# The node sum of a graph's values: seven adds on GpSimd and one product instead of eight, in the next feed-forward

## The chip, the cores and the metric

One NeuronCore of a Trainium2 chip runs the whole program. The metric is device time of one execution in microseconds (us); the median of three runs is taken. The engines are TensorE (PE; its weight loads are PEld), VectorE (DVE), ScalarE (ACT), GpSimd (POOL) and SyncE (SP), which issues the DMAs.

## What is computed

Eight graphs of 1024 nodes with 256 features go through a three-layer graph transformer (L0), and then through one graph-attention layer (L1). Cut to what matters here:

```python
h = relu(layernorm(x))
x = x + L0(h, adj)                 # 3 layers: masked attention, layernorm, feed-forward, layernorm
h = relu(layernorm(x))
# L1:
Wh = h @ W
e = leaky_relu((Wh @ a1)[:, :, None] + (Wh @ a2)[:, None, :])
e = where(adj == 0, -1e9, e)
h_prime = softmax(e, axis=2) @ Wh
x = x + elu(h_prime)
```

In L1 a node may have no edge at all. All its scores are then equal, and its row of the softmax is a plain mean over the 1024 nodes. The kernel needs for this the sum of `Wh` over all nodes of a graph, a row of 256 numbers that stands in every partition: the node sum. It is added where a node has no edge.

## The kernel before, in words

The nodes of a graph lie in 8 tiles of 128 partitions. The work is 32 steps, one layer of one graph each, in the order of the table `ORDER`: steps of L0 are feed-forward steps (`ffn_step`), steps of L1 are `gat_step`. Each engine has its own program, which walks through the steps in the same order; inside a step the order is written out by hand by tables (`prep_tables`) and conditions on `t` (the tile, 0 to 7) and `n` (the feed-forward iteration, 0 to 15). The engines wait for one another through semaphores. No scheduler moves anything.

A feed-forward step has two parts. In the first, for `t` in 0 to 7, TensorE makes `aggregate` (8 products of f32, 128x257, each recorded in two halves, so x16 in the trace) into the banks `OB`, and VectorE makes `residual1` (L1105, L1109) and the LN1 statistics. GpSimd turns statistics into factors (`ln_rstd`, L621 to L629), ScalarE normalises (L822), and after tiles 3, 5 and 7 TensorE transposes pairs of tiles (L1636). In the second, for `n` in 0 to 15, TensorE makes `hidden` (6 products, up-projection, two iterations ahead) and `second` (12 products, down-projection into `OB`), ScalarE the GELU (L853) and its upper half (L858), and the lower half is made by VectorE for even `n` (L1242) and by GpSimd for odd `n` (L657). At the end VectorE adds the residual (`residual2`, L1122) from `OB`, which frees the banks for the first `aggregate` of the next step, makes the LN2 statistics (L1095, L1098), and splits the columns of scores (L1168 to L1174). GpSimd makes the LN2 factors and `affine` (a multiply L644 and an add L646 per tile, 128x256 f32); those of tiles 4 to 7, `tail`, stand at the start of its next step.

In the shadow of a step other work is done: scores of the next step (`unit` on TensorE, 4 products with `nms`; `score` on VectorE, L1228; exponentials on ScalarE, L864), masks, row maxima (L1204), and the preparation of a graph for L1 (`GAT_AT`: the step in which it is prepared). For graph 0 that is step 5, for graphs 1 to 5 steps 8, 12, 16, 20 and 24, for graph 6 step 28, for graph 7 the `gat_step` 29. `gat_product` makes `Wh`, `gat_values` writes it to `xx` (signal `wv_done`), `scores` on VectorE (L1146 and L1151) reduce it with `a1` and `a2`: two inputs in SBUF, 128x256, one instruction each.

The node sum of a graph is `gat_colsum` on TensorE: eight products of a matrix of ones with the eight tiles of `xx`, f32, summed in the bank `TP`. It stands at `n == 14`, ahead of `second(k, 14)`. `gat_sum` on VectorE (L1284) copies it into `csum`, after the LN2 statistics at the end of the step. It is read by `elu_a` (L1299) in the `gat_step` of that graph, at step 6 for graph 0 and one to five steps after the preparation for the others.

Of the kernel before, what the change touches and what calls it, by code (L numbers as in the profile page):

```python
# [37 lines left out]
BATCH, N, D = 8, 1024, 256  # L38
LAYERS, FF = 3, 1024
NT = N // P  # L40
# [46 lines left out]
GAT_FFN_LATE = {5}  # L87

# [102 lines left out]
def build(nc, x, adj, attn_w, attn_b, W1, b1, W2, b2, g1, beta1, g2, beta2, gatW, gata, out):  # L191
# [10 lines left out]
    with ctx:  # L202
# [143 lines left out]
        cs_done = sem("cs_done")  # L346
        wct_done = sem("wct_done")
# [243 lines left out]
        def _(pool):  # L591
# [89 lines left out]
            def ffn_step(k):  # L681
# [29 lines left out]
                for n in range(NF):  # L711
# [24 lines left out]
                    if n == 13:  # L736
                        ln_rstd(LN2, i, 1)
                        affine(LN2, k, 0)
                        affine(LN2, k, 1)
                affine(LN2, k, 2)  # L740
                affine(LN2, k, 3)

            def gat_step(k):
# [30 lines left out]
                for t in range(NT):  # L774
                    final(g, t)

# [310 lines left out]
        def _(dve):  # L1087
# [300 lines left out]
            def ffn_step(k):  # L1388
# [22 lines left out]
                for n in range(NF):  # L1411
# [32 lines left out]
                    if k + 2 in AHEAD:  # L1444
                        if n == 8:
                            columns(k + 2)
                        if n == 10:
                            cT_copy(k + 2)
                            constants(k + 2)
                        mask_rows(k + 2, MAX_AHEAD.get(8 + n, ()))  # L1450
                    if n == 10:
                        statistics2(k, 0)
# [38 lines left out]
                if gat is not None:  # L1491
                    gat_sum(gat)
# [11 lines left out]
            def gat_step(k):  # L1504
                gat = GAT_AT.get(k)
                for t in range(NT):
# [18 lines left out]
                    for u in prep_tables(k)["units"].get(t, ()):  # L1525
                        score(k + 1, u)
                    if k == 30 and t == 6:
                        gat_sum(7)
# [62 lines left out]
        def _(pe):  # L1591
# [184 lines left out]
            def gat_colsum(g):  # L1776

                pe.wait_ge(wv_done, 4 * g + 4)
                pe.wait_ge(*tp_after[-1])
                for jt in range(NT):  # L1780
                    ins = mm(TPf[:, 0:D], onesf[:, :], xx[:, g % 3, jt, 0:D], jt == 0, jt == NT - 1)
                ins.then_inc(cs_done, 1)
                tp_after.append((csc_done, g + 1))
# [13 lines left out]
            def ffn_step(k):  # L1797
# [12 lines left out]
                for n in range(NF):  # L1810
# [21 lines left out]
                    if gat is not None and n == 14:  # L1832
                        gat_colsum(gat)
# [5 lines left out]
            def gat_step(k):  # L1839
                gat = GAT_AT.get(k)  # L1840
                for t in range(NT):
# [4 lines left out]
                    if gat is not None:  # L1846
                        if t >= 5:
                            gat_product(gat, t - 5)
                        if t >= 4:
                            gat_transpose(gat, t - 4)  # L1850
                    if k == 30 and t == 5:
                        gat_colsum(7)
# [47 lines left out]
```

## Time and profile before

| | us |
|---|---|
| median of three runs (2563.61 to 2567.0) | 2563.79 |
| the profiled execution | 2558.94 |
| its span, first to last instruction | 2557.2 |
| TensorE busy | 2299.9 |
| VectorE busy | 1839.7 |
| ScalarE busy | 1579.6 |
| GpSimd busy | 1274.2 |

The profile is of one execution, so its durations are compared with its own 2558.94 us. Timeline rows give the start and the duration of a group of like instructions in us from the span's start; a bracket at the end is the time for which the engine stood idle before it, and what ended that. Rows of the chain of waits give start, duration and what held the end of the program there. The mean granted clock of TensorE over the span is 0.985 of full speed.

### The profile page before, as it was taken

Reading aid. Unit: us, or ns where it says so; the run is one execution under the profiler, and the core shown is the slowest. Engines: PE = TensorE matmul, PEld = TensorE weight load, DVE = VectorE, ACT = ScalarE, POOL = GpSimd, SP = SyncE. Lnnn points to the kernel's source line nnn. Section 1 sums busy time; section 2 is a strip of 40 time slices with the busy share of each in tenths; the row PEclk is TensorE's granted clock in tenths of the full one; section 3 lists DMA queues with packets and bytes.
Section 4 is the critical chain, followed back from the end, with each engine's and each line's share of the span. In section 5 each row is a group of like instructions: output and inputs, shape, how many; then the busy total and the mean of one; then the engine's idle time right before and its main releaser. Section 6 shows DMA issues by size and latency. Waiting matters only on the chain.

```text
span 2557.2 us, 41683 instructions
## 1 busy us (share of the span) xinstructions
PE 2299.9 (90%) x14721; PEld 1726.5 (68%) x14721; DVE 1839.7 (72%) x4915; ACT 1579.6 (62%) x2426; POOL 1274.2 (50%) x2199
## 2 busy tenths in 40 slices
PE   5899999997899998999989999899997999999977
PEld 4566666766666766766767767667675677677666
DVE  7676678567677776776877768768677677666775
ACT  5466566655566665665756657565666657666654
POOL 4455455653275453654446533655545456546621
PEclk9999999998999999999999999999999999999998
DMA  6212021101120112100211102111031010001000
GB/s 220 101 42 87 9 87 42 59 1 50 60 89 5 38 50 91 59 18 25 83 59 59 42 3 89 54 54 42 33 109 44 15 42 9 14 29 26 20 23 25
DMA packets 66222, 128.57 MB, mean 50 GB/s; under 512 B 12985, under 2 KB 53213, under 8 KB 62942
## 3 DMA queue, kind: packets, MB, share of 16 engines
q1 hardware_dynamic: 66014, 125.90, 14.8%
q8 instruction: 117, 1.92, 0.3%
q14 instruction: 91, 0.75, 0.1%
HBM read 111.20 MB, written 14.68 MB: 49 GB/s over the span
## 4 chain that ended last, share of the span: by engine, by line
PE 53%; DVE 23%; ACT 8%; issue 8%; POOL 7%; DMA 1%; DVEq 0%; SPq 0%; POOLq 0%; ACTq 0%
PE OB L1595 36%; PE FBB L1595 10%; DVE pw L1228 5%; PE RB L1595 3%; DVE mj L1204 3%; DVE junk L1146 3%; ACT nms L881 2%; DVE st L1095 2%; PE TH L1595 2%; DVE xc L1122 1%; ACT gT L858 1%; POOL rs L626 1%; POOL xc L644 1%; DVE junk L1151 1%; DVE gT L1242 1%
## 5 line engine op out<-in xcount | busy, mean ns | idle before, releaser
L1595 PE MATMUL OB<-xx,pw 128*128 128x257 f32 x4096 | 960.9, 389 | 29.5 <-DVE xc L1122 12.6
L1595 PEld LDWEIGHTS OB<-xx,pw 128*128 128x128 f32 x4096 | 771.5, 193 | 170.0 <-DVE xc L1122 18.9
L1595 PE MATMUL FBB<-hT,wb 128*128 128x512 f16 x2304 | 560.3, 381 | 52.2 <-DVE gT L1242 38.1
L1595 PE MATMUL OB<-wb,gT 128*128 128x256 f16 x4608 | 574.3, 275 | 28.9 <-DVE xc L1122 17.2
L1595 PEld LDWEIGHTS OB<-wb,gT 128*128 128x128 f16 x4608 | 449.6, 99 | 168.1 <-POOL gT L657 22.0
L657 POOL TENSOR_TENSOR gT<-g,gT 128x512 f16<-128x512 f32 x192 | 226.9, 1182 | 538.0 <-ACT gT L858 536.8
L1595 PEld LDWEIGHTS FBB<-hT,wb 128*128 128x128 f16 x2304 | 212.7, 98 | 260.2 <-DVE gT L1242 45.3
L864 ACT ACTIVATE pw<-pw,sj 128x512 f32<-128x512 f32 x512 | 336.4, 712 | 67.5 <-DVE pw L1228 66.7
L1228 DVE SCALAR_TENSOR_TENSOR pw<-r2s,sj,RB 128x512 f32<-128x512 f32 x452 | 319.9, 739 | 43.1 <-PE RB L1595 42.9
L822 ACT ACTIVATE xc<-xc,nb,rs 128x256 f32<-128x256 f32 x384 | 212.6, 590 | 196.0 <-POOL nb L629 196.0
L644 POOL TENSOR_TENSOR xc<-xc,gb 128x256 f32<-128x256 f32 x384 | 293.8, 765 | 16.1 <-ACT xc L822 16.0
L1242 DVE TENSOR_TENSOR gT<-FBB,gT 128x512 f16<-128x512 f32 x192 | 131.9, 687 | 228.6 <-ACT gT L858 228.0
L881 ACT ACTIVATE nms<-nm,cc 128x1024 bf16<-128x1024 bf16 x256 | 282.7, 1135 | 7.6 <-DVE cc L1219 7.6
L1204 DVE CUSTOM_DVE_ANT_0 mj<-RB,nm 128x1024 bf16<-128x1024 f32 x224 | 266.2, 1215 | 12.6 <-PE RB L1595 12.6
L621 POOL TENSOR_SCALAR ve<-mv 128x2 f32<-128x2 f32 x256 | 59.4, 232 | 415.9 <-DVE mv L1098 403.7
L1595 PE MATMUL RB<-identb,nms 128*128 128x128 bf16 x1808 | 163.5, 225 | 76.0 <-DVE pw L1228 62.5
L853 ACT ACTIVATE FBB<-FBB,wc 128x512 f32<-128x512 f32 x192 | 125.7, 654 | 146.7 <-PE FBB L1595 146.1
L853 ACT ACTIVATE g<-FBB,wc 128x512 f32<-128x512 f32 x192 | 130.6, 680 | 110.8 <-PE FBB L1595 110.8
L1595 PEld LDWEIGHTS RB<-identb,nms 128*128 128x128 bf16 x1808 | 124.5, 100 | 106.4 <-DVE pw L1228 84.3
L1105 DVE RECIPROCAL rden<-OB 128x1 f32<-128x1 f32 x192 | 31.9, 166 | 225.7 <-PE OB L1595 225.3
L626 POOL TENSOR_TENSOR rs<-ve,mhalf 128x2 f32<-128x2 f32 x256 | 181.7, 710 | 21.3
L1151 DVE CUSTOM_DVE_ANT_0 junk<-xx,aw 128x256 bf16<-128x256 f32 x256 | 169.5, 662 | 0.0
(127 smaller groups left out, 2663.6 us busy)
## 6 DMA issues: line engine op xcount, KB each, us to landing
wb<-w_scratch SPq DMA_DIRECT2D x19, 2048.0 KB, 8.2
adjst<-in_adj SPq DMA_DIRECT2D x56, 512.0 KB, 4.1
xx<-in_x SPq DMA_DIRECT2D x16, 512.0 KB, 5.6
nm<-in_L_gnn_W SPq DMA_DIRECT2D x6, 1024.0 KB, 8.4
gb<-in_L_gnn_g SPq DMA_DIRECT2D x48, 128.0 KB, 2.9
adjst<-in_x SPq DMA_DIRECT2D x6, 1024.0 KB, 11.2
out_x<-adjst SPq DMA_DIRECT2D x48, 128.0 KB, 1.7
pw<-in_adj SPq DMA_DIRECT2D x4, 1024.0 KB, 10.3
```

The source lines that it names most:

```text
L626: pool.tensor_tensor(out=rs[:, kind, c], in0=ve[:, kind, c], in1=mhalf[:, :], op=ALU.pow)\
L644: pool.tensor_tensor(out=v, in0=v, in1=gb[:, 0, :], op=ALU.mult).then_inc(mul_done[kind], 1)
L657: pool.tensor_tensor(out=gT[:, i % GRING, 1, :], in0=g32[:, :], in1=gT[:, i % GRING, 0, :], op=ALU.subtract).then_inc(glo_odd, 1)
L822: act.activation(dst, src, ACT.Relu if kind in (LNR, LNG) else ACT.Identity, bias=nb[:, kind, t:t + 1], scale=rs[:, kind, t:t + 1])\
L853: act.activation(dst, src, ACT.Gelu, bias=b1c[:, layer(k), f:f + 1], scale=1.0 / W_SCALE)\
L864: act.activation(v, v, ACT.Exp, bias=sj2[:, q % 2, jt:jt + 1]).then_inc(exp_done, 1)
L881: act.activation(nms[:, it, :], nm[:, slot(q), it, :], ACT.Identity, bias=cc[:, it:it + 1])\
L1151: dve.tensor_tensor_reduce(out=junk[:, 1, :], in0=src, in1=aw[:, l, 1, :], scale=1.0, scalar=0.0, op0=ALU.mult, op1=ALU.add, accum_out=sc[ ...
L1204: dve.tensor_tensor_reduce(out=mj[:, n % 2, :], in0=row_bank(q)[:, :], in1=nm[:, g % 3, t, :], scale=1.0, scalar=-3e38, op0=ALU.add, op1=A ...
L1228: dve.scalar_tensor_tensor(out=pw[:, jt, half], in0=r2s[:, half], scalar=sj8[:, q % 2, jt:jt + 1], in1=b, op0=ALU.max, op1=ALU.add).then_i ...
L1242: dve.tensor_tensor(out=gT[:, i % GRING, 1, :], in0=FB[i % 2][:, :], in1=gT[:, i % GRING, 0, :], op=ALU.subtract).then_inc(glo_even, 1)
L1595: return pe.matmul(o, lhsT, rhs, start=first, stop=last)
```

## The change

For graphs 0 to 6 the sum over the eight tiles is made elementwise: a new `node_sum` on GpSimd adds the eight tiles of `xx` into `csum` with seven adds of 128x256 f32, each waiting for the one before (`part_done`). TensorE then makes one product of the ones with `csum` instead of eight with `xx`, and VectorE copies the result over `csum` as before. Graph 7 keeps the eight products.

`node_sum` stands at the end of GpSimd's feed-forward step, behind `affine` of tiles 2 and 3 and ahead of the `tail` of the next step. The product and the copy move to the following step, to `n == 3` on TensorE and `n == 4` on VectorE (for graph 6, which is followed by a `gat_step`, to `t == 2` and `t == 3` of step 29). For graph 0, whose `gat_step` comes right behind, the product and the copy stay where they are in step 5, and the adds stand at `n == 9`.

```diff
+SUM_AT = {k if k in GAT_FFN_LATE else k + 1: g for k, g in GAT_AT.items() if g < 7}
...
+                    if n == 9 and k in GAT_FFN_LATE:
+                        node_sum(gat)
                 affine(LN2, k, 2)
                 affine(LN2, k, 3)
+                if gat is not None and k not in GAT_FFN_LATE:
+                    node_sum(gat)
...
+            def node_sum(g):
+
+                acc = csum[:, g % 2, :]
+                v = xx[:, g % 3, :, 0:D]
+                for t in range(1, NT):
+                    if t == 1 or t % 2 == 0:
+                        pool.wait_ge(wv_done, 4 * g + t // 2 + 1)
+                    if t > 1:
+                        pool.wait_ge(part_done, 7 * g + t - 1)
+                    pool.tensor_tensor(out=acc, in0=v[:, 0, :] if t == 1 else acc, in1=v[:, t, :],
+                                       op=ALU.add).then_inc(part_done, 1)
...
+                    if n == 4 and k in SUM_AT and k not in GAT_FFN_LATE:
+                        gat_sum(SUM_AT[k])
...
-                if gat is not None:
+                if k in GAT_FFN_LATE:
                     gat_sum(gat)
...
+                    if k == 29 and t == 3:
+                        gat_sum(6)
...
-                pe.wait_ge(wv_done, 4 * g + 4)
+                if g < 7:
+                    pe.wait_ge(part_done, 7 * g + 7)
+                else:
+                    pe.wait_ge(wv_done, 4 * g + 4)
                 pe.wait_ge(*tp_after[-1])
-                for jt in range(NT):
-                    ins = mm(TPf[:, 0:D], onesf[:, :], xx[:, g % 3, jt, 0:D], jt == 0, jt == NT - 1)
+                if g < 7:
+                    ins = mm(TPf[:, 0:D], onesf[:, :], csum[:, g % 2, :], True, True)
+                else:
+                    for jt in range(NT):
+                        ins = mm(TPf[:, 0:D], onesf[:, :], xx[:, g % 3, jt, 0:D], jt == 0, jt == NT - 1)
...
-                    if gat is not None and n == 14:
-                        gat_colsum(gat)
+                    if k in SUM_AT and n == (14 if k in GAT_FFN_LATE else 3):
+                        gat_colsum(SUM_AT[k])
...
+                    if k == 29 and t == 2:
+                        gat_colsum(6)
```

The new lines shift the numbers of the lines behind them (L1595 becomes L1617, L646 becomes L648).

TensorE, end of step 12 and start of step 13, before: down-projections (`OB<-wb,gT`), a score unit (`RB<-identb,nms`), the node sum (`TP<-xx,onesf`), the first aggregate (`OB<-xx,pw`).

```order
L1595 MATMUL OB<-wb,gT 128x256 x12
L1595 MATMUL RB<-identb,nms 128x128 x4
L1595 MATMUL TP<-xx,onesf 128x256 x8
L1595 MATMUL OB<-wb,gT 128x256 x24
L1595 MATMUL OB<-xx,pw 128x257 x8
L1697 MATMUL TP<-identb,c 64x128
```

The same place after.

```order
L1617 MATMUL OB<-wb,gT 128x256 x12
L1617 MATMUL RB<-identb,nms 128x128 x4
L1617 MATMUL OB<-wb,gT 128x256 x24
L1617 MATMUL OB<-xx,pw 128x257 x8
L1719 MATMUL TP<-identb,c 64x128
```

The node sum's products are gone from between the score unit and the last two down-projections.

TensorE, `n` 2 to 4 of step 13, after.

```order
L1617 MATMUL OB<-wb,gT 128x256 x12
L1617 MATMUL RB<-identb,nms 128x128 x8
L1617 MATMUL TP<-csum,onesf 128x256
L1617 MATMUL FBB<-hT,wb 128x512 x6
L1617 MATMUL OB<-wb,gT 128x256 x12
L1617 MATMUL RB<-identb,nms 128x128 x8
```

The one product now stands there ahead of an up-projection (`FBB<-hT,wb`); nothing else is moved.

GpSimd, end of step 12 and start of step 13, after: low half, `affine` of tiles 2 and 3, then the LN2 factors of tiles 4 and 5.

```order
L659 TENSOR_TENSOR gT<-g,gT 128x512
L646 TENSOR_TENSOR xc<-xc,gb 128x256
L648 TENSOR_TENSOR xx<-xc,gb 128x256
L646 TENSOR_TENSOR xc<-xc,gb 128x256
L648 TENSOR_TENSOR xx<-xc,gb 128x256
L792 TENSOR_TENSOR csum<-xx 128x256
L792 TENSOR_TENSOR csum<-csum,xx 128x256 x6
L623 TENSOR_SCALAR ve<-mv 128x2
L625 TENSOR_SCALAR ng<-mv 128x2
L628 TENSOR_TENSOR rs<-ve,mhalf 128x2
L631 TENSOR_TENSOR nb<-ng,rs 128x2
```

The seven adds (L792) are new, between `affine` and the factors.

## Rows read from the trace of the kernel before

**Rows 1.** The page, busy us, share of the span and instructions by engine.

```profile
PE 2299.9 (90%) x14721; PEld 1726.5 (68%) x14721; DVE 1839.7 (72%) x4915; ACT 1579.6 (62%) x2426; POOL 1274.2 (50%) x2199
```

**Rows 2.** Chain of waits, steps 12 to 13: start us, us, what.

```profile
1146.76 0.68 DVE xc L1122 x2
...
1147.48 3.74 PE OB L1595 x16
```

**Rows 3.** TensorE timeline, steps 12 to 13: start us, us, engine, line, operation.

```profile
1140.86 3.67 PE L1595 MATMUL TP<-xx,onesf 128*128 128x256 f32 x16
1144.38 2.78 PE L1595 MATMUL OB<-wb,gT 128*128 128x256 f16 x24
1147.48 3.74 PE L1595 MATMUL OB<-xx,pw 128*128 128x257 f32 x16 [0.32 <-DVE xc L1122]
...
1163.34 0.60 PE L1636 MATMUL TH<-ident,xc 128*128 128x128 f32 x4
```

**Rows 4.** VectorE timeline, steps 12 to 13; none of the rows left out has idle time.

```profile
1138.41 1.40 DVE L1228 SCALAR_TENSOR_TENSOR pw<-r2s,sj,RB 128x512 f32<-128x512 f32 x2
...
1145.12 0.94 DVE L1151 CUSTOM_DVE_ANT_0 junk<-xx,aw 128x256 bf16<-128x256 f32 x1
...
1145.99 0.41 DVE L1146 CUSTOM_DVE_ANT_0 junk<-xx,aw 128x256 bf16<-128x256 f32 x1
...
1146.68 1.41 DVE L1122 SCALAR_TENSOR_TENSOR xc<-OB,xc 128x256 f32<-128x256 f32 x4
```

**Rows 5.** GpSimd timeline, steps 12 to 13.

```profile
1141.13 1.34 POOL L657 TENSOR_TENSOR gT<-g,gT 128x512 f16<-128x512 f32 x1
...
1144.98 0.79 POOL L646 TENSOR_TENSOR xx<-xc,gb 128x256 f32<-128x256 f32 x1
1149.05 0.19 POOL L621 TENSOR_SCALAR ve<-mv 128x2 f32<-128x2 f32 x1 [3.28 <-DVE mv L1098]
...
1159.82 0.19 POOL L629 TENSOR_TENSOR nb<-ng,rs 128x2 f32<-128x2 f32 x1
```

**Rows 6.** Timelines of GpSimd and TensorE, step 5.

```profile
568.38 1.16 POOL L657 TENSOR_TENSOR gT<-g,gT 128x512 f16<-128x512 f32 x1 [3.53 <-ACT gT L858]
...
582.49 1.16 POOL L657 TENSOR_TENSOR gT<-g,gT 128x512 f16<-128x512 f32 x1 [2.66 <-ACT gT L858]
...
571.91 1.47 PE L1595 MATMUL OB<-wb,gT 128*128 128x256 f16 x12
```

**Rows 7.** Timelines of GpSimd and VectorE, steps 28 to 29.

```profile
2410.40 0.79 POOL L646 TENSOR_TENSOR xx<-xc,gb 128x256 f32<-128x256 f32 x1
2416.56 0.19 POOL L621 TENSOR_SCALAR ve<-mv 128x2 f32<-128x2 f32 x1 [5.37 <-DVE mv L1098]
...
2414.18 1.42 DVE L1122 SCALAR_TENSOR_TENSOR xc<-OB,xc 128x256 f32<-128x256 f32 x4 [2.22 <-PE OB L1595]
```

**Rows 8.** ScalarE timeline, steps 12 to 13.

```profile
1143.17 6.24 ACT L864 ACTIVATE pw<-pw,sj 128x512 f32<-128x512 f32 x10
...
1160.04 1.09 ACT L822 ACTIVATE xc<-xc,nb,rs 128x256 f32<-128x256 f32 x2 [2.75 <-POOL nb L629]
```

**Rows 9.** Timelines of ScalarE and TensorE, step 25.

```profile
2086.77 1.09 ACT L822 ACTIVATE xc<-xc,nb,rs 128x256 f32<-128x256 f32 x2 [3.65 <-POOL nb L629]
...
2088.22 0.60 PE L1636 MATMUL TH<-ident,xc 128*128 128x128 f32 x4
```

**Rows 10.** TensorE after idle gaps; the last row is 413 to 417 us: busy, clock, DMA.

```profile
412.59 5.42 PE L1595 MATMUL OB<-xx,pw 128*128 128x257 f32 x16 [3.45 <-DVE xc L1122]
...
2442.67 1.48 PE L1595 MATMUL TH<-gw,wb 128*128 128x256 f16 x12 [3.35 <-DVE wb L1279]
...
413.00:417.00 4.00, 4.00 (x13) 0.57 0.71 303
```

**Rows 11.** TensorE timeline, step 13, `n == 4`.

```profile
1195.09 0.40 PE L1595 MATMUL RB<-identb,nms 128*128 128x128 bf16 x4 [0.40 <-DVE pw L1228]
```

**Rows 12.** Chain of waits, step 25, `n == 3`.

```profile
2117.84 1.29 PE FBB L1595 x6
```

More of the change, by code:

```diff
@@ L346, in build @@
         cs_done = sem("cs_done")
+        part_done = sem("part_done")
         wct_done = sem("wct_done")
```

## The prediction

> **What bounds the kernel now.** I read the page's busy shares first, then the chain of waits, then the four engines' timelines at each place that the change touches. TensorE is busy 90% of the span and the other engines 50 to 72% [rows 1], so the first look says: take work from TensorE, and the span shrinks by it. The chain contradicts this at the places in question. At the end of step 12 (the same picture stands at steps 8, 16, 20 and 24) the chain runs through VectorE: it ends with two `residual2` products and only then enters TensorE with the first aggregate of step 13 [rows 2]. The TensorE timeline shows the eight products of the node sum at 1140.86, the last two down-projections at 1144.38 and the aggregate at 1147.48, after a wait of 0.32 us for `residual2` [rows 3]. VectorE had no idle moment in the 8.3 us before that `residual2`; it was working through scores and units [rows 4]. So the node sum lies in the shadow of VectorE. What ends last there is VectorE's list, not TensorE's.
>
> **The change part by part.**
>
> *Products removed.* Eight products start at 1140.86 and the next work at 1144.38, so eight take 3.52 us and one 0.44 us [rows 3]; seven sums lose 7 x 3.08 = 21.6 us of TensorE work. At steps 8, 12, 16, 20 and 24 the down-projections then end near 1144.0 instead of 1147.2 in step 12's times (the last of them waits for GpSimd's low half, out at 1142.5 [rows 5]), but `residual2` still starts when VectorE comes to it, 1146.68 [rows 4]. Gain: 0 of 3.08 us, five times. At step 5 the last down-projection waits for GpSimd's subtraction, which itself waited 2.66 us for ScalarE [rows 6]: gain 0. Only at step 28 was VectorE idle, 2.22 us, until TensorE delivered [rows 7]; there is something to gain there, and the next part takes it back.
>
> *Adds put on GpSimd.* Seven dependent adds of 128x256 f32. The nearest row is the second half of `affine`, same shape and same wait for the one before: 0.79 us [rows 5], 0.80 us from start to start. Seven take 5.6 us, 39 us in all seven sums. In step 12 they start at 1145.8 and end at about 1151.4. They have two effects.
>
> First, VectorE's last two score reductions. With GpSimd at work such a reduction takes 0.94 us, with GpSimd idle 0.42 us [rows 4]: the one at 1145.12 falls in GpSimd's `affine`, which ends at 1145.77 [rows 5], the one at 1145.99 comes after it. The held one ends 0.29 us after GpSimd's operation: it waits until that is through. Today the last two are free because GpSimd has just run dry; now the adds stand there. Two reductions go from about 0.35 to 0.87 us each from start to start: +0.52 x 2, of which I take 0.93 us since the first add may start late. This is on the chain: `residual2` moves from 1146.68 to 1147.6 and the aggregate from 1147.48 to 1148.4. Bounds: 0, if VectorE slips in before the first add and the second, and 1.9 us, if both wait for a whole operation of 1.34 us, the longest of GpSimd's here [rows 5]. I take 0.93, five times: **+4.7 us**.
> The Trainium skill, GPSIMD Engine Reference, section Specifications, says that GpSimd's SBUF interfaces are shared with VectorE and that instructions with two SBUF inputs or in a two-port mode contend. The reductions have two SBUF inputs, and the trace agrees (0.94 against 0.42). `residual2` reads one operand from PSUM: by the rule the adds leave it alone and the sum stays as it is; were its first two products held like the reductions, another 0.9 us would come in at five steps, +4.7, and no row shows one beside an operation of GpSimd.
>
> Second, GpSimd's tail. Today the LN2 statistics of tiles 4 to 7 are taken up at 1149.05 after 3.28 us idle [rows 5]; now at about 1151.5, +2.5 us. Everything up to the first LN1 factors of step 13 (their last instruction at 1159.82) is back to back, so these shift by as much, and ScalarE's normalise from 1160.04 to 1162.5, ending 1163.6 [rows 8]. TensorE wants the result at 1163.34 [rows 3], but is itself late by the 0.9 us above and what follows. Cost 0 at steps 8 to 20, with 0.7 us of cover after the contention alone and 2.3 us after the next loss too. In step 25 no spreads stand between the aggregates; TensorE comes to the transpose at 2088.22 and ScalarE ends at 2087.86 [rows 9]: a shift of 2.4 us with 0.36 us of cover makes TensorE 2.1 us late. That is less than the 2.6 us below, so it adds nothing unless that is missing. At step 28 `residual2` could start some 1.3 us earlier (2.22 less the 0.9 of contention), but GpSimd's adds run from about 2411.2 to 2416.8, where the LN2 factors start at 2416.56 today [rows 7]; the chain goes through them. +0.3 us.
>
> *The hole in TensorE.* TensorE's 3.5 us of sum are replaced by idling: from about 1144.0 to 1148.4, 4.4 us. The trace has the very same spot once, at the end of an earlier feed-forward: 3.45 us idle until `residual2`, then the first aggregate in 5.42 us instead of 3.74, at a mean granted clock of 0.57, so mostly at 1.2 instead of 2.4 GHz [rows 3, 10]. It also has a gap of 3.35 us after which the products ran at full speed (12 in 1.48 us) [rows 10]. The gap here is longer than both, so I take the fall, 5.42 - 3.74 = 1.68 us, bounds 0 and 2.0 (a fall that covers more of it). Five times: **+8.4 us**. The Trainium skill, TensorE: Matmul & The Clock Gate, section Why this matters for your kernels, warns against idle gaps between bursts because the clock falls to half; the row agrees. With its rule the sum is 14.1 us, without it 6.8.
>
> *One product and the copy, moved.* In steps 9, 13, 17, 21 the product (0.44 us) stands ahead of an up-projection after which TensorE waits 0.40 us for VectorE [rows 11]: covered but for 0.04. In step 25 that stretch is TensorE work on the chain [rows 12]: +0.4 us. VectorE's copy of `csum` (0.3 us) goes from the chain's side to a place where the chain is on TensorE, 0; in step 29 it lands among VectorE's critical row work, +0.3 us.
>
> *Step 5.* The adds start at about 564.8, where GpSimd idles 3.53 us until 568.38 [rows 6]; they overrun by 2.1 us, the subtraction ends at 571.6 instead of 569.5, and TensorE wants it at 571.91. Cost 0. A slower clock in the thinner end of that step could cost up to 0.9; I take 0.
>
> Sum: 4.7 + 8.4 + 0.4 + 0.3 + 0.3 = **+14.1 us**. On the profiled execution (span 2557.2, 2558.94 with what lies around it) that is 2573.0. The median of the runs shown is 4.9 us above that execution, so the predicted median is 2563.8 + 14.1 = **2577.9 us**.
>
> **The rivals.**
> *One of the two losses is missing.* Without the clock's fall: 4.7 + 1.1 (the late transpose of step 25 now shows) + 1.0 = +6.8 us, 2570.6. Without the contention: 4 x 1.68 + 2.1 + 1.0 = +9.8 us, 2573.6. For it: gaps of a little over 3 us went both ways [rows 10].
> *Neither (no change).* The adds wait for one another through a semaphore, and VectorE may pass in the gaps; TensorE's gap is then near 3.4 us, as long as the ones of both kinds. Left are the late transpose and the moved pieces: 2.1 + 1.0 = +3.1 us, 2566.9. Against it: `affine` has the same waits, and held the reduction all the same.
> *TensorE was the bound after all (faster).* If VectorE's list shrank with TensorE's, the aggregate could go as soon as the exponentials allow: ten take 6.24 us from 1143.17 [rows 8], so the eighth is out at 1148.2 and the aggregate ends near 1148.6, 2.6 us sooner than today. 5 x 2.6 + 2.2 at step 28 - 0.7 = -14.5 us, 2549.3. It decides if VectorE waits for TensorE anywhere in 1138.4 to 1146.7; no row shows it.
> *The tail gets later still.* If each add took more than 1.13 us, the LN1 factors would pass the 2.3 us of cover and stall the transposes in every step; at 1.34 us each, +7.4 us more: 2585.
>
> **How the numbers follow.** Forecast 0.48; one loss missing 0.23; neither 0.15; faster 0.09; later tail 0.05. A measurement of this kernel tells about 0.2% (5.1 us) from no change. So slower 0.76, same 0.15, faster 0.09. The range leaves out the faster case, the lower part of "neither" and the late tail: 2566 to 2584; its upper end is the forecast with both bounds, 2.0 for each fall of the clock (+1.6) and 1.9 for each contention (+4.8).
>
> **What would show it.** Right: TensorE idle about 4.4 us before the first aggregate of steps 9, 13, 17, 21, 25, that aggregate near 5.4 us long with a granted clock well under 1; the last two reductions before `residual2` at about 0.9 us; seven GpSimd adds near 0.75 us; LN2 factors of tiles 4 and 5 taken up about 2.5 us later after `residual2` than now; the busy sum of TensorE about 20 us lower at a longer span. Wrong: `residual2` at steps 8 to 24 starting sooner after the last GELU than today (then TensorE had been the bound), an aggregate of 3.74 us after the gap, or adds that leave the reductions at 0.42 us.

## The result

The changed kernel is slower: 2577.23 us in the median of five runs (2573.5 to 2584.09) against 2563.61 us for the kernel before (five runs, 2556.87 to 2567.0), a ratio of 1.0061, 95% interval 1.0043 to 1.008. The profiled execution took 2576.79 us, its span is 2575.1 us, 17.9 more than before, at a mean granted clock of TensorE of 0.978 against 0.985. One further execution of the kernel before, 3336.99 us at a mean granted clock of 0.668, is in none of the numbers here.

The page of the changed kernel, busy us by engine, answers to [rows 1].

```profile
PE 2291.3 (89%) x14623; PEld 1714.8 (67%) x14623; DVE 1854.9 (72%) x4915; ACT 1580.4 (61%) x2426; POOL 1307.6 (51%) x2248
```

TensorE lost 98 recorded halves of products, 21.6 us of work, but its busy time fell by 8.6 us only: the rest came back, most of it as slower products. GpSimd has 33.4 us more, VectorE 15.2 us more with the same number of instructions.

TensorE's timeline at the end of step 12 and the start of step 13 (start, duration, operation, idle time ahead of it) answers to [rows 3]; the third row is the next step of the same kind, cut by the window after three of its products, and the last one the transpose of step 13.

```profile
1143.18 1.48 PE L1617 MATMUL OB<-wb,gT 128*128 128x256 f16 x12 [0.19 <-POOL gT L659]
1149.07 6.34 PE L1617 MATMUL OB<-xx,pw 128*128 128x257 f32 x16 [4.40 <-DVE xc L1140]
...
1459.81 1.65 PE L1617 MATMUL OB<-xx,pw 128*128 128x257 f32 x3 [4.40 <-DVE xc L1140]
...
1167.53 0.60 PE L1658 MATMUL TH<-ident,xc 128*128 128x128 f32 x4
```

The wait for `residual2` is 4.40 or 4.41 us in all five steps where it was 0.32 or 0.33. The aggregate behind it takes 6.46, 6.34, 6.27 and 6.22 us in steps 9, 13, 17 and 21, instead of 3.74; in step 25, whose row holds four aggregates in one, it is 15.85 instead of 14.16 us. The view by stretches gives the clock of that gap and of that aggregate (bounds, length, then busy us of PE, PEld, DVE, ACT, POOL, granted clock, DMA share, GB/s).

```profile
1144.66:1149.07 4.41, 0.01 (x1) 0.00 (x1) 4.41 (x12) 4.41 (x8) 3.97 (x7) 0.83 0.79 253
1149.07:1155.41 6.34, 6.34 (x17) 4.85 (x17) 4.90 (x22) 2.26 (x5) 5.47 (x11) 0.58 0.37 156
```

A granted clock of 0.83 in the gap and 0.58 behind it says that the clock falls from 2.4 to 1.2 GHz inside the gap, and that most of the aggregate runs on the lower level. (In step 25 the whole gap was granted 1.00, and the fall came within the aggregate.) The reason for the longer gap is in VectorE's and GpSimd's timelines of the same place, which answer to [rows 4] and [rows 5].

```profile
1145.76 0.93 DVE L1169 CUSTOM_DVE_ANT_0 junk<-xx,aw 128x256 bf16<-128x256 f32 x1
...
1146.63 0.85 DVE L1164 CUSTOM_DVE_ANT_0 junk<-xx,aw 128x256 bf16<-128x256 f32 x1
...
1147.41 0.93 DVE L1169 CUSTOM_DVE_ANT_0 junk<-xx,aw 128x256 bf16<-128x256 f32 x1
...
1148.27 1.41 DVE L1140 SCALAR_TENSOR_TENSOR xc<-OB,xc 128x256 f32<-128x256 f32 x4
...
1146.38 0.82 POOL L792 TENSOR_TENSOR csum<-xx 128x256 f32<-128x256 f32 x1
1147.34 4.66 POOL L792 TENSOR_TENSOR csum<-csum,xx 128x256 f32<-128x256 f32 x6
1152.08 0.21 POOL L623 TENSOR_SCALAR ve<-mv 128x2 f32<-128x2 f32 x1
```

The last two reductions end at 1148.27 after 1.64 us; before they took 0.69 us from 1145.99 to 1146.68. Each lasts until about 0.3 us after the GpSimd operation beside it has ended. `residual2`, which reads one operand from PSUM, takes 1.41 us beside the adds, as it did without them. ScalarE normalises at 1163.31 and TensorE wants the result at 1167.53, so GpSimd's later tail stalls nothing:

```profile
1163.31 1.09 ACT L840 ACTIVATE xc<-xc,nb,rs 128x256 f32<-128x256 f32 x2 [1.84 <-POOL nb L631]
```

The steps repeat every four, so the distance between the first aggregates of steps 8, 12, 16 and 20 measures the loss of one occurrence. Before it is 307.2 us three times; after it is 310.9, 310.7 and 310.7, that is +3.5 to +3.7 us. The profiled spans differ by these parts: from the start to 530 us -3.2 (work ahead of the first change), to step 8 +0.1, step 8 to 20 +10.7, to step 25 +7.1, step 25 +2.1, steps 26 to 28 -1.3, step 29 to the end +2.3; together +17.9.

### The profile page after: what moved, and what is told of

Read it like the earlier page. It is cut to its first block, busy times and chain, and to the rows that moved or that the text cites. A ratio compares the mean times of both kernels' runs of the same rounds, so it can differ in the third digit from the quotient of the medians.

```text
span 2575.1 us, 41557 instructions
## 1 busy us (share of the span) xinstructions
PE 2291.3 (89%) x14623; PEld 1714.8 (67%) x14623; DVE 1854.9 (72%) x4915; ACT 1580.4 (61%) x2426; POOL 1307.6 (51%) x2248
## 4 chain that ended last, share of the span: by engine, by line
PE 53%; DVE 23%; issue 8%; ACT 8%; POOL 7%; DMA 1%; DVEq 0%; SPq 0%; POOLq 0%; ACTq 0%
PE OB L1617 36%; PE FBB L1617 10%; DVE pw L1246 5%; PE RB L1617 3%; DVE mj L1222 3%; DVE junk L1164 3%; ACT nms L899 2%; DVE st L1113 2%; PE TH L1617 2%; POOL xc L646 1%; DVE junk L1169 1%; DVE xc L1140 1%; ACT gT L876 1%; POOL rs L628 1%; DVE gT L1260 1%
## 5 line engine op out<-in xcount | busy, mean ns | idle before, releaser
L1617 PE MATMUL OB<-xx,pw 128*128 128x257 f32 x4096 | 971.4, 392 | 52.9 <-DVE xc L1140 35.2
L1617 PEld LDWEIGHTS OB<-xx,pw 128*128 128x128 f32 x4096 | 778.5, 195 | 196.7 <-DVE xc L1140 41.5
L1617 PE MATMUL FBB<-hT,wb 128*128 128x512 f16 x2304 | 562.1, 382 | 51.2 <-DVE gT L1260 38.4
L1617 PE MATMUL OB<-wb,gT 128*128 128x256 f16 x4608 | 574.6, 275 | 32.0 <-DVE xc L1140 17.1
L1617 PEld LDWEIGHTS OB<-wb,gT 128*128 128x128 f16 x4608 | 449.2, 99 | 172.2 <-POOL gT L659 24.8
L1617 PEld LDWEIGHTS FBB<-hT,wb 128*128 128x128 f16 x2304 | 213.2, 98 | 260.7 <-DVE gT L1260 45.9
L646 POOL TENSOR_TENSOR xc<-xc,gb 128x256 f32<-128x256 f32 x384 | 293.5, 764 | 16.2 <-ACT xc L840 16.1
L1617 PE MATMUL RB<-identb,nms 128*128 128x128 bf16 x1808 | 163.8, 225 | 78.0 <-DVE pw L1246 61.6
L1617 PEld LDWEIGHTS RB<-identb,nms 128*128 128x128 bf16 x1808 | 124.5, 100 | 108.6 <-DVE pw L1246 83.3
## 6 DMA issues: line engine op xcount, KB each, us to landing
adjst<-in_x SPq DMA_DIRECT2D x6, 1024.0 KB, 10.9
```

The costliest lines, as they stand in the source:

```text
L646: pool.tensor_tensor(out=v, in0=v, in1=gb[:, 0, :], op=ALU.mult).then_inc(mul_done[kind], 1)
L1617: return pe.matmul(o, lhsT, rhs, start=first, stop=last)
```

## The experiments

Ten kernels were run. The table has the ratio to the kernel before, run on the same chip in the same rounds, and the three distances just named. Its last two columns rest on a fit. Each execution comes with its time and its mean granted clock. Over the 190 executions of these kernels whose clock is on record, one straight line of 1.58 us for each 0.001 of clock and one offset for each kernel describe the times, with a rest of 1 to 2 us. It splits the difference of the mean time to the kernel before (79 executions, mean clock 0.9825) into what stands at equal clock and what goes with the clock. A regression shows what goes together, not what causes it, and the clock is given to three digits only; it is used as a second reading beside the rows. The two columns don't separate the causes cleanly either: e3, in which the contention is gone from the chain, still stands at +5.8 us at equal clock.

| kernel | ratio, 95% interval | three distances, us | at equal clock, us | with the clock, us |
|---|---|---|---|---|
| before | 1 | 307.2, 307.2, 307.2 | 0 | 0 |
| after | 1.0061 (1.0043 to 1.008) | 310.9, 310.7, 310.7 | +6.3 | +10.3 |
| e1_adds_only | 1.0029 (1.0017 to 1.0041) | 308.2, 309.8, 308.2 | +7.3 | +1.5 |
| e2_no_adds | 1.0017 (1.0005 to 1.0029) | 310.1, 308.7, 309.0 | +1.4 | +4.9 |
| e3_adds_later | 1.0059 (1.0044 to 1.0074) | 309.1, 309.3, 310.5 | +5.8 | +10.9 |
| e4_scores_late | 1.0067 (1.0052 to 1.0082) | 310.5, 310.5, 310.6 | +6.7 | +7.4 |
| e5_fill_hole | 1.0026 (1.0015 to 1.0037) | 308.2, 308.2, 308.2 | +6.9 | +0.3 |
| e6_before_scores_late | 1.0032 (1.002 to 1.0044) | 308.9, 308.8, 308.9 | +8.4 | -2.0 |
| e7_adds_later_scores_late | 1.0013 (1.0001 to 1.0025) | 305.6, 307.1, 307.1 | -5.4 | +6.4 |
| e8_adds_later_fill | 1.0015 (1.0003 to 1.0027) | 307.6, 307.5, 307.5 | +1.8 | +1.0 |
| e9_last_graph_before | 1.0004 (0.999 to 1.0017) | 305.7, 305.6, 305.6 | -4.5 | +5.5 |
| e10_product_in_wait | 1.0013 (1.0002 to 1.0025) | 308.2, 306.7, 307.9 | -1.6 | +6.2 |

### The adds alone, and the hole alone

e1_adds_only keeps the eight products and puts the adds on GpSimd beside them.

```diff
+                if gat is not None and k not in GAT_FFN_LATE and gat < 6:
+                    node_sum(gat)
...
+                acc = csum[:, (g + 1) % 2, :]
```

> The kernel before with GpSimd's adds alone: for graphs 0 to 5 the seven adds stand where the change puts them, but go into the unused half of csum and nobody reads them; TensorE keeps its eight products at n 14. My theory (VectorE is what the first aggregate waits for, and the adds hold its last two score reductions): residual2 0.9 to 1.0 us later at steps 8, 12, 16, 20, 24, those reductions at 0.85 to 0.94 us instead of 0.42, TensorE idle only about 1.2 us before the aggregate, so that it keeps 3.74 us; the time 5 to 8 us above the kernel before. Rival A (adds are harmless, the whole loss is the clock): within 2 us of before. Rival B (adds are the whole loss, through the late LN factors): 13 to 18 us above before, with TensorE waiting at the transposes of every following step.

e2_no_adds is the changed kernel without the adds.

```diff
-                if gat is not None and k not in GAT_FFN_LATE:
-                    node_sum(gat)
...
-                    ins = mm(TPf[:, 0:D], onesf[:, :], csum[:, g % 2, :], True, True)
+                    ins = mm(TPf[:, 0:D], onesf[:, :], xx[:, g % 3, 0, 0:D], True, True)
```

> The changed kernel without the adds: GpSimd adds nothing for graphs 0 to 6 and the one product reads tile 0 of the values alone, so the node sums are not computed. 21.6 us of TensorE products are gone and nothing stands in their place. My theory: residual2 starts when it does before the change, TensorE stands idle about 3.4 us, and the time gains nothing: between 0 (clock stays) and +13 us (it falls at five steps and the aggregate takes 5.4 to 6.3 us). Rival (TensorE's work is the bound): 14 to 20 us below the kernel before, residual2 sooner.

TensorE's timeline at the first aggregate of step 13, first of e1, then of e2.

```profile
1154.30 3.74 PE L1612 MATMUL OB<-xx,pw 128*128 128x257 f32 x16 [1.27 <-DVE xc L1139]
```

```profile
1154.54 5.15 PE L1613 MATMUL OB<-xx,pw 128*128 128x257 f32 x16 [3.45 <-DVE xc L1136]
```

The two losses come apart. With the adds and with the products, the wait is 0.32 + 0.95 = 1.27 us and the aggregate runs at full speed: +0.96 us per distance, twice; the middle one has a fall of the clock elsewhere. Without both, the wait is 3.45 us, and the aggregates take 5.15 to 6.56 us: +1.5 to +2.9 us per distance, all of it clock. Neither loss hangs on the other. The profiled execution of e2 was the slowest of its twelve, 2576.47 us against a median of 2568.49, so its prices for the clock lie on the high side. In the medians e1 is 8.9 us above the kernel before and e2 5.8.

### Work put into the hole

e5_fill_hole is the changed kernel, adds and single product included; eight products whose result is not read stand behind the last down-projection.

```diff
+            def fill(g):
+                pe.wait_ge(*tp_after[-1])
+                for jt in range(NT):
+                    mm(TPf[:, 0:D], onesf[:, :], xx[:, g % 3, jt, 0:D], jt == 0, jt == NT - 1)
...
                     second(k, n)
+                if early:
+                    fill(gat)
```

> The changed kernel with eight products of the ones with the value tiles behind the last down-projection of steps 8, 12, 16, 20, 24 and 28, whose result nobody reads: 3.5 us of work in TensorE's 4.4 us hole. My theory (half or more of the loss is the clock that falls in the hole): the first aggregate of steps 9, 13, 17, 21, 25 back at 3.74 us from 6.3, residual2 where it is in the changed kernel, 10 to 13 us below the changed kernel, so 4 to 7 us above before. Rival (the aggregate is slow for another reason, waiting for exponentials or for operands that GpSimd and VectorE contend for): the aggregate stays near 6.3 us and the time within 2 us of the changed kernel, or above it by what the products cost.

```profile
1144.08 3.62 PE L1617 MATMUL TP<-xx,onesf 128*128 128x256 f32 x16
1148.66 3.74 PE L1617 MATMUL OB<-xx,pw 128*128 128x257 f32 x16 [0.97 <-DVE xc L1140]
```

More work made the kernel faster. TensorE does 3.6 us more in each of six steps, the aggregate is back at 3.74 us, the distances fall from 310.7 to 308.2 us, and the median falls by 8.2 us, from 2577.2 to 2569.0. The two kernels were not run in the same rounds; by their ratios to the kernel before the gain is 9.0 us, with an uncertainty of some 5 us. Both are less than the 10 to 13 us expected, though 6.3 us above the kernel before is within the 4 to 7 of the same text, and the sixth filling is part of the reason: the stretch from step 28 to 29 is 2.6 us longer than in the changed kernel (100.8 against 98.1 us). The prediction had 8.4 us for the hole. What is left, 1.04, 1.06 and 1.02 us per distance, is mostly the contention, which it put at 0.93.

### The adds moved on, into the next feed-forward

e3_adds_later makes the adds of graphs 1 to 5 at `n` 5 and 7 of the next feed-forward, the product at `n` 8 and the copy at `n` 9.

```diff
+                    if k in SUM_AT and k not in GAT_FFN_LATE and n in (5, 7):
+                        node_sum(SUM_AT[k], range(1, 5) if n == 5 else range(5, NT))
...
-                if gat is not None and k not in GAT_FFN_LATE:
+                if gat == 6:
                     node_sum(gat)
```

> The changed kernel with the adds of graphs 1 to 5 moved to the next feed-forward, four behind GpSimd's subtraction at n 5 and three at n 7 (about 5 us idle each in the trace of before); the product goes to n 8 and the copy to n 9. My theory: the last two reductions are back at 0.42 us and residual2 is 0.95 us earlier than in the changed kernel, the idle of TensorE before the aggregate shrinks from 4.4 to about 3.4 us; if the clock still falls, 4 to 6 us below the changed kernel (+9 to +12 on before), if it doesn't, 12 to 16 us below it (within 3 us of before). Rival (the place of the adds does not matter, TensorE's hole is all): the same time as the changed kernel within 2 us.

```profile
1153.42 5.42 PE L1619 MATMUL OB<-xx,pw 128*128 128x257 f32 x16 [3.45 <-DVE xc L1142]
...
2091.56 14.16 PE L1619 MATMUL OB<-xx,pw 128*128 128x257 f32 x64 [3.45 <-DVE xc L1142]
```

The wait is that of e2, 3.45 instead of 4.40 us: the contention is gone from the chain. The aggregates of steps 9, 13, 17 and 21 are 5.25 to 6.70 us long, and two of the three distances are 1.4 and 1.8 us shorter than in the changed kernel. The second row is step 25: the same wait of 3.45 us, and four aggregates in 14.16 us, exactly as before the change, at a granted clock of 1.00. The median is no better than that of the changed kernel, 2578.9 us in six executions, so the expected 4 to 6 us less did not come, and the number is the one that the rival named, the same time within 2 us; in the profiled one the stretch from step 29 on is 147.1 us long against 144.5 after and 142.2 before, which gives the gain back. Why this kernel lies 10 us above e2_no_adds, where the distances differ by less than 1 us in the mean, was not settled.

e8_adds_later_fill is e3 with the unread products of e5.

> The run with the adds in the next feed-forward (label e3), and in addition the eight unread products behind the last down-projection. That run kept a gap of 3.45 us before the aggregate and aggregates of 5.25 to 6.7 us; the products fill the gap. If contention and clock are the two causes and nothing else is, no loss is left but the moved product: within 4 us of the kernel before, aggregates 3.74 us, residual2 where it was before the change, 10 to 14 us below e3. Rival (the moved product and copy are what e3 lost): 3 us or less below e3.

It took 2564.6 us, 14.3 us less than e3 and 3.1 us more than the kernel before; the distances are 0.33 us above before. With both losses taken away, but by moving the adds and by paying for the hole with useless work, the kernel is nearly back where it was, and no further: the node sum had been in a shadow.

### Taking the reductions out of the way

If VectorE's list is what ends last, shortening it ahead of `residual2` should pay where TensorE has room. In e4_scores_late (the changed kernel) and e6_before_scores_late (the kernel before) the four reductions of tiles 6 and 7 stand behind the LN2 statistics.

```diff
-                        if n >= 8:
+                        if 8 <= n < 14:
                             scores(GAT_STEP[gat], n - 8)
...
                 statistics2(k, 2)
                 statistics2(k, 3)
+                if gat is not None and early:
+                    scores(GAT_STEP[gat], 6)
+                    scores(GAT_STEP[gat], 7)
```

> The changed kernel with one edit on VectorE: the scores of the last two tiles of the prepared graph (four reductions, until now at n 14 and 15, ahead of residual2) stand behind the LN2 statistics, ahead of the column split. My theory (VectorE's list, not TensorE, held the first aggregate): residual2 now starts as soon as TensorE delivers, about 3 to 4 us sooner than in the changed kernel; the hole in TensorE closes to under 1 us, the aggregate no longer takes 6.3 us; it is paced by the exponentials. The four reductions now stand beside the adds (0.87 us each) and ahead of the column split, for which TensorE waits at its transpose, so part of the gain goes there. Time 12 to 20 us below the changed kernel, from 5 below to 2 above the kernel before. Rival (something else than VectorE's list holds residual2): within 3 us of the changed kernel.

> The kernel before with the same edit on VectorE alone: four reductions behind the LN2 statistics, eight products and no adds on GpSimd. With 3.5 us of node sum still ahead of the last down-projections, TensorE and VectorE finished about together at this place. My theory: residual2 and the aggregate at most 0.3 us sooner, and the later column split may cost that again: within 3 us of the kernel before. Rival (the edit on VectorE is worth the whole of what the next run shows, and TensorE's products nothing): 8 us or more below the kernel before.

TensorE's timeline of e4 at the start of step 13, with one row of VectorE between.

```profile
1142.21 4.59 PE L1620 MATMUL OB<-xx,pw 128*128 128x257 f32 x16 [0.34 <-DVE xc L1140]
...
1146.02 0.94 DVE L1164 CUSTOM_DVE_ANT_0 junk<-xx,aw 128x256 bf16<-128x256 f32 x1
...
1149.36 0.32 PE L1722 MATMUL TP<-identb,c 128*64 128x128 bf16 x1 [2.55 <-DVE c L1192]
1149.61 6.66 PE L1620 MATMUL OB<-xx,pw 128*128 128x257 f32 x16
```

The first part came true: the aggregate starts 93.0 us after that of step 12 instead of 97.1 and waits 0.34 us. The four deferred reductions now run beside the adds and take 3.1 us, where four that run free take 1.4. Behind them VectorE splits the score column `c` that TensorE transposes next, and TensorE waits 2.55 us for it. The clock falls in that wait, and the *second* aggregate takes 6.66 us. Of the 4.1 us won at one wait 3.9 are lost again: from the start of the first aggregate to the end of the second e4 takes 14.1 us, the changed kernel 10.2. The parts are 2.55 for the wait, 2.92 for the slow second aggregate and 0.85 for the first (4.59 us at full clock; that ScalarE's exponentials pace it is argued from their rate, not shown), less the 2.6 us that the changed kernel loses in its own first aggregate. The expected gain of 12 to 20 us did not come. In e6, where TensorE still has its products, the start is only 0.13 us earlier, and the same transpose waits 1.20 us: +1.65 us per distance, nothing in return. Its median is 8.4 us above the kernel before, where at most 3 were expected.

e7_adds_later_scores_late does both moves, so that adds and deferred reductions do not meet.

> The changed kernel with both edits: adds of graphs 1 to 5 in the next feed-forward (n 5 and 7), product at n 8, and the four reductions behind the LN2 statistics. Nothing holds residual2 but TensorE, the reductions run at 0.42 us, the column split is ready in time. The aggregate starts near the end of the last down-projection and is paced by the exponentials; the next aggregate starts 2 to 2.6 us sooner than before the change, at five steps, less 0.4 us each for the product on the way. My theory: 6 to 12 us below the kernel before (0.25 to 0.45%), below both kernels. Rival (the place was bound by something further on, so that a sooner aggregate gains nothing): within 3 us of before.

```profile
1137.15 4.59 PE L1622 MATMUL OB<-xx,pw 128*128 128x257 f32 x16 [0.34 <-DVE xc L1142]
1141.94 0.24 PE L1724 MATMUL TP<-identb,c 128*64 128x128 bf16 x1 [0.20 <-DVE c L1194]
1142.11 3.74 PE L1622 MATMUL OB<-xx,pw 128*128 128x257 f32 x16
...
1206.50 0.53 PE L1622 MATMUL RB<-identb,nms 128*128 128x128 bf16 x4 [0.26 <-DVE pw L1248]
...
1207.21 2.74 PE L1622 MATMUL FBB<-hT,wb 128*128 128x512 f16 x6
```

This is the order in which the removed products are worth something. The transpose waits 0.20 us, and the first distance is 305.6 us, 1.6 below before. The median is 12 to 14 us below the changed kernel, by ratios and by medians, but it misses the expectation of 6 to 12 us under the kernel before: 1.0013, and not faster. At equal clock it stands at -5.4 us; +6.4 us go with the clock, which now falls at other places. The largest loss is at the end: the stretch from step 29 on takes 149.3 us, 7.1 more than before the change, with a wait of 4.63 us for the copy of the sum in it; step 28 gives back 3.5 of them. One of the new falls is shown: six up-projections in 2.74 instead of 1.46 us in step 13, a stretch granted 0.65:

```profile
1206.96:1211.40 4.44, 4.44 (x21) 2.38 (x21) 3.17 (x14) 1.32 (x2) 0.00 (x0) 0.65 0.00 0
```

### The last graph as before, and the product put elsewhere

e9_last_graph_before is e7 with graph 6 put back (`g < 6` in the place of `g < 7`, its scores and eight products in their old places); up to step 27 it has the same instructions as e7. e10_product_in_wait moves e9's single product behind two score units at `n` 9.

> The kernel e7_adds_later_scores_late (adds and product of graphs 1 to 5 in the next feed-forward, two tiles' scores behind the statistics) with graph 6 put back as in the kernel before: eight products and the copy in step 28, no adds, scores in their old place. Theory A (what is left of the loss of e7 sits in the last feed-forward and in step 29, where TensorE waits 4.63 us for the copy of the node sum, and the stretch from the first aggregate of step 28 to the end is 3.5 us longer than before): 3 to 4 us faster than e7, about 2560 us median, 1 to 2 us under the kernel before; the last two stretches within 0.5 us of before. Rival B (the other copy and transposes of step 29 wait for something else, and the sum is only the one that came last): no faster than e7, 2563 us or more.

> e9_last_graph_before with one change: the single product of graphs 1 to 5 stands not ahead of hidden 12 of the next feed-forward but later, between two broadcasts of masked maxima, where TensorE waits 1.19 us for a score of VectorE; VectorE's and GpSimd's order is that of e9. Theory A (in e7 the product of 0.49 us runs on the path, the wait of 1.19 us stands behind it, and the clock falls there for 3.4 us in each of steps 16, 20 and 24, for 1.4 us each): the product goes into the wait, that clock fall is gone, and each of four steps is 0.5 to 1.9 us shorter: 2 to 8 us faster than e9, about 2555 us median, 0.2 to 0.4% under the kernel before. Rival B (the clock falls there whatever stands in the wait, or the score that ends it is later by what the product was): within 1 us of e9.

TensorE's timeline of e9 in step 13, at the place where e7 lost its clock.

```profile
1207.59 0.40 PE L1618 MATMUL RB<-identb,nms 128*128 128x128 bf16 x4 [1.19 <-DVE pw L1246]
1208.25 0.40 PE L1618 MATMUL RB<-identb,nms 128*128 128x128 bf16 x4 [0.26 <-DVE pw L1246]
...
1208.75 1.47 PE L1618 MATMUL FBB<-hT,wb 128*128 128x512 f16 x6
```

The same instructions with the same waits, 1.19 and 0.26 us, and here the clock holds: distances of 305.6 us instead of 307.1. So the instructions and their waits alone don't decide whether the clock falls. In the median e9 is at 1.0004, no different from the kernel before and from e7. Rival B of its text fits better: e7's wait of 4.63 us for the copy of the sum in step 29 is gone, yet from step 29 on e9 took 145.0 us, where the same instructions took 142.2 us in the kernel before. Each has its own falls of the clock there.

For e10 the text on record names steps 16, 20 and 24; the falls of e7 are in steps 13, 17 and 21. Its expected gain did not come.

```profile
1214.93 0.65 PE L1618 MATMUL TP<-csum,onesf 128*128 128x256 f32 x2
1217.35 0.40 PE L1618 MATMUL RB<-identb,nms 128*128 128x128 bf16 x4 [1.77 <-DVE pw L1246]
```

The product is in the wait, but the wait behind it is now 1.77 us where it was 1.19: rival B's second reason, a score that comes later by about what the product takes. e10 is 2.4 us above e9 in the median, more than the 1 us that rival B allowed, and in no distance better; the one distance in which the clock did not fall, 306.7 us, is 1.1 us longer than that of e9. What makes up the 1.1 us was not settled.

No kernel beats the kernel before; e9 can't be told from it in time.

## Why the prediction was right

The forecast was 2577.9 us, the median is 2577.23, inside the range of 2566 to 2584, on the side that had 0.76. The terms, one by one:

**What bounds.** Right. `residual2` starts after an unbroken list of VectorE, not when TensorE delivers, in all five steps; 21.6 us of products left and none of these five steps became shorter. e8 shows the same from the other side: with useless products in the hole the distances are within 0.34 us of before.

**Contention.** Right in mechanism and size: 0.93 us forecast, 0.95 between the two reductions' rows, 0.96 (e1) and 1.02 to 1.06 (e5) in the distances. The doubt about a held `residual2` could have been settled from the trace of the kernel before: of its 192 instructions of `residual2`, 110 have an operation of GpSimd beside them for more than half of their time, and their median is 0.41 us, as is that of the others. That agrees with the Trainium skill, GPSIMD Engine Reference, section Specifications, by which instructions with two SBUF inputs contend with GpSimd; `residual2` has one in PSUM.

**The clock.** Right in mechanism, but the price was too low. The gap is 4.40 us as forecast, and the loss behind it is 2.72, 2.60, 2.53 and 2.48 us in steps 9 to 21, not 1.68, each above the stated bound of 2.0; in step 25 it is 1.69. Together that is 12.0 us where the sum had 8.4. The forecast took the price from a gap of 3.45 us, and e2 and e3, which have just that gap, show what was wrong with it: 5.15, 5.20, 5.25, 5.42, 5.42, 6.56, 6.63 and 6.70 us for the same aggregate in steps 9 to 21, and in step 25 a loss of 3.0 us in e2 and of none in e3. One row had been one draw from a spread of 0 to 3.0 us. That filling the hole gives back 8.2 us in the median (8.4 forecast) does not confirm the term: the uncertainty is some 5 us, and 2.6 us of step 28 are taken off in it.

**GpSimd's tail.** Right in effect. GpSimd takes up the LN2 factors 2.4 us later, counted from its last low half, which lies ahead of the adds (10.3 us behind the start of it instead of 7.9). The prediction's sign said "after `residual2`", and counted so it is 1.4 us, 3.8 instead of 2.4, since `residual2` moved by 0.95 itself. TensorE reaches the transpose of step 13 (1167.53) after ScalarE has ended (1164.4). In step 25 the late tail was to show, at 1.1 us, only where the clock's loss is missing. e1 is that case:

```profile
2100.87 0.66 PE L1653 MATMUL TH<-ident,xc 128*128 128x128 f32 x4 [1.11 <-ACT xc L839]
```

TensorE waits 1.11 us there for ScalarE, and the distance from step 25 to 26 is 81.0 us in e1 where it was 79.7.

**The moved product and copy.** The distance from step 25 to 26 grew by 2.1 us, of which the slow aggregate is 1.7; 0.4 us was forecast for the product, and 0.4 is left. In e3 and e8, where neither a slow aggregate nor a late tail stands in it, the same distance is 0.5 us longer than before.

**Step 28.** Wrong in sign: +0.3 us was forecast, and the stretch from step 28 to 29 is 1.3 us *shorter* in the profiled execution, 98.1 against 99.5 us. VectorE did use the room that the missing products left, and the adds did not take it back. The price stands in the next step, which the forecast put at +0.3 us: TensorE waits 3.50 us there for the copy of `csum`, and step 29 to the end is 2.3 us longer.

```profile
2430.59 5.43 PE L1617 MATMUL OB<-xx,pw 128*128 128x257 f32 x16 [2.37 <-DVE xc L1140]
...
2455.20 1.09 PE L1779 MATMUL TP<-ident,wb 128*128 128x128 f32 x4 [3.50 <-DVE csum L1302]
```

The first row shows something else that the sum did not have, a sixth fall: this aggregate took 5.43 us instead of 3.74, after a wait of 2.37 us; in e3 it took 3.74 us after 2.38. And the wait for `csum` is not all loss, since the kernel before waits in the same stretch for 1.20 and 3.35 us for others. How the 2.3 us divide stays open: e3 took 147.1 us there without the slow aggregate, and e9 145.0 us with the order of before.

**Step 5.** Right: the subtraction at 566.88 and the down-projections behind it wait for nothing new.

```profile
562.32 4.61 POOL L792 TENSOR_TENSOR csum<-csum,xx 128x256 f32<-128x256 f32 x6
566.88 1.16 POOL L659 TENSOR_TENSOR gT<-g,gT 128x512 f16<-128x512 f32 x1
```

**What the sum did not have.** Besides the terms, the profiled execution has some 2.7 us more of falls about 1930 to 1980 us than the profiled one of before, and 3.2 us less at the start. Such parts cancelled about. The profiled executions are 17.9 us apart, the medians 13.6, because the profiled one of before lay 4.9 us under its median. That the forecast came within 0.7 us of the median is luck in good part: the clock's term was 3.6 us too small at the five places, and the interval of the ratio alone is 4.7 us wide to each side. The fit, which averages over executions, gives +6.3 us at equal clock and +10.3 us with it, where the forecast's terms without and with the clock were 5.7 and 8.4 us.

**The rivals.** "One loss is missing" had the right prices for one half: contention alone was put at +6.8 us, and e5 stands at +6.6 in the ratio, e1 at +7.4. The other half, clock alone, was put at +9.8 us, more than it turned out: e2, which has it without the adds, stands at +4.4 us in the ratio; its step 28 is 2.3 us shorter than before, which that price did not have. "TensorE was the bound" is refuted by the start of `residual2`. What it hoped for needs VectorE's list to be shortened as well, and e4 to e9 show how little is behind it: the next waits are those for the score column and for the row maxima.

## What to carry to other kernels

An engine busy 90% of the span can still be in another's shadow where the work is removed; look at what releases the instruction behind it. Before work is taken off TensorE, look whether a gap of a few microseconds opens there: the clock can make the next products longer, here by 1.7 to 2.7 us, and that counts in full where the removed ones had cost nothing. Before work is put on an idle GpSimd, look at which VectorE instructions with two inputs in SBUF stand beside it, and whether they are on the chain.

## What was not expected of the hardware

- The time of one kernel follows the mean granted clock from one execution to the next: the kernel before took 2555.7 us at 0.987 and 2566.7 us at 0.978, on one chip in the same rounds. A single profile is one draw; here those of before and of e9 lay 5 and 10 us under their medians.
- Waits of 1.19 us cost nothing in e9 and 1.5 us in e7, in the same instructions. A price read from one row after one gap has that much spread, and removing one gap moves the falls elsewhere: in e7 three sit in step 13, 17 and 21 where the kernel before has none. The Trainium skill, TensorE: Matmul & The Clock Gate, section Why this matters for your kernels, warns of idle gaps between bursts; the traces agree for gaps of 3.45 and 4.4 us in 14 of the 15 cases of e2, e3 and the changed kernel ahead of steps 9, 13, 17, 21 and 25; in the fifteenth, e3 ahead of step 25, no fall followed a gap of 3.45 us. For shorter gaps they leave it open: a fall followed 2.37 us of waiting in the changed kernel and none followed 2.38 us in e3.
- A GpSimd operation does not slow a two-input reduction in proportion; it holds it. The reductions end about 0.3 us after the operation beside them, so 0.41 us becomes 0.85 to 0.96 us beside an add, and 1.37 us beside the subtraction of 1.34 us. In the trace of the kernel before, 274 of the 329 reductions that begin beside an operation of GpSimd end 0.28 to 0.30 us after it. Casts of 128x16 were held as well, 0.50 instead of 0.17 us in e4 and 0.62 us in the changed kernel (off the chain there), though they read one input only.
